# GpSimd's share of scaling duT: another instruction, and 1.5 chunks a step in the third to seventh segment

## The reference, cut to what matters

```python
dA = jnp.exp(delta[..., None] * A)
dBu = delta[..., None] * Bm[:, :, None, :] * u[..., None]
def step(h, inp):
    dA_t, dBu_t, C_t = inp
    h = dA_t * h + dBu_t
    y = jnp.einsum('bdn,bn->bd', h, C_t)
    return (h, y)
```

## Time and profile before

| | us |
|---|---|
| median of 3 runs (699.59 to 702.44) | 699.82 |
| span of the profiled execution | 716.2 |
| first product L564 starts | 60.4 |
| third segment's first product | 170.5 |
| eighth segment's first product | 461.5 |
| last product ends | 515.7 |

### The profile page before, as it was taken

The page is one execution under the profiler, slowest core; times in us unless marked ns, Lnnn a source line. Parts: engine busy times, 40 slices in busy tenths (PEclk is TensorE's granted clock), DMA queues, the critical chain, the costliest instruction groups (busy, mean ns, idle before and its releaser), DMA issues.

```text
span 716.2 us, 14511 instructions
## 1 busy us (share of the span) xinstructions
PE 619.3 (86%) x4435; PEld 514.5 (72%) x4435; DVE 551.1 (77%) x1170; ACT 542.8 (76%) x1023; POOL 512.8 (72%) x479
## 2 busy tenths in 40 slices
PE   3878789989979988998998995878798878899995
PEld 3435757857857767776786784767688878899994
DVE  4357689899999999989999999899954663555553
ACT  3268989989998998998998998889655543565650
POOL 3147969878899899899899999868735445444440
PEclk9999999999999999999999999899999999999997
DMA  7030534445734633553344533596112222222535
GB/s 231 2 118 2 139 89 151 112 127 166 233 103 133 170 103 102 147 156 105 99 121 132 141 101 102 156 238 163 39 47 58 59 56 65 62 67 62 166 123 184
DMA packets 65197, 82.93 MB, mean 116 GB/s; under 512 B 6961, under 2 KB 55153, under 8 KB 61025
## 3 DMA queue, kind: packets, MB, share of 16 engines
q1 hardware_dynamic: 59648, 70.78, 36.3%
q0 software_dynamic: 4320, 9.12, 3.8%
q10 hardware_dynamic: 1152, 2.10, 0.8%
HBM read 52.19 MB, written 29.78 MB: 114 GB/s over the span
## 4 chain that ended last, share of the span: by engine, by line
PE 40%; ACT 37%; DVE 11%; issue 8%; another core or an unknown queue 2%; DMA 2%; ACTq 0%; DVEq 0%; SPq 0%
PE psum L594 25%; PE psum L598 15%; ACT S L1019 13%; ACT dA L1027 12%; DVE ring L1383 4%; ACT L958 1%; ACT xn L923 1%; DMA ring<-results 1%; ACT L1027 1%; ACT soft L951 1%; ACT soft L950 1%; ACT soft L958 1%; ACT soft L955 1%; ACT hT L905 1%
## 5 line engine op out<-in xcount | busy, mean ns | idle before, releaser
L564 POOL TENSOR_TENSOR ring<-ring,Cb 128x1024 f32<-128x1024 f32 x128 | 279.9, 2188 | 37.2 <-DVE ring L1383 36.8
L598 PEld LDWEIGHTS psum<-ident,S 128*128 128x128 f32 x1024 | 118.7, 142 | 112.7 <-issue 66.4
L598 PE MATMUL psum<-ident,S 128*128 128x128 f32 x1024 | 158.8, 279 | 42.5 <-POOL S L547 13.7
L1019 ACT ACTIVATE S<-duT,BT 128x256 f32<-128x256 f32 x384 | 166.5, 502 | 25.3 <-DVE duT L1123 22.6
L1027 ACT ACTIVATE dA<-delta,A 128x512 f32<-128x512 f32 x256 | 178.7, 716 | 8.6 <-DVE ring L1383 8.5
L598 PE MATMUL psum<-ident,ring 128*128 128x128 f32 x1088 | 159.7, 278 | 5.4 <-DMA ring<-results 5.3
L1383 DVE TENSOR_TENSOR_SCAN ring<-dA,state,psum 128x512 f32<-128x512 f32 x128 | 157.7, 1265 | 1.0 <-PE psum L598 0.4
L1383 DVE TENSOR_TENSOR_SCAN ring<-dA,psum 128x512 f32<-128x512 f32 x128 | 150.1, 1206 | 8.8 <-PE psum L598 8.2
L586 POOL DMA_INDIRECT results<-xn,result_at x71 | 69.0, 972 | 92.2 <-DVE xn L1516 76.5
L598 PEld LDWEIGHTS psum<-ident,ring 128*128 128x128 f32 x1088 | 129.0, 144 | 6.7 <-DMA ring<-results 5.9
L594 PE MATMUL psum<-uT,S 128*128 128x128 f32 x852 | 109.7, 279 | 1.6 <-DVE uT L1494 1.2
(11 more groups left out here) (226 smaller groups left out, 739.0 us busy)
## 6 DMA issues: line engine op xcount, KB each, us to landing
Cb<-c_rows SPq DMA_DIRECT2D x32, 1024.0 KB, 6.0
token_rows<-zeros SPq DMA_DIRECT2D x64, 272.0 KB, 6.7
uT<-token_rows SPq DMA_DIRECT2D x71, 68.0 KB
ring<-results SPq DMA_DIRECT2D x8, 512.0 KB
xT<-in_xT SPq DMA_DIRECT2D x4, 512.0 KB, 5.4
out_T<-xT ACTq DMA_DIRECT2D x8, 256.0 KB, 2.3
stage<-in_xT SPq DMA_DIRECT2D x6, 256.0 KB, 7.8
gateup_w<-in_gate SPq DMA_DIRECT2D x1, 1408.0 KB, 10.3
```

The lines of the kernel that those rows point to most:

```text
L564: nc.gpsimd.tensor_tensor(ring[:, k % RING, :, 0:BANK], ring[:, k % RING, :, 1:], Cb[:, group_ % 2, own, :].unsqueeze(1).to_broadcast([P, ...
L598: return nc.tensor.matmul(out, block_in, ident[at, at], is_transpose=True, start=start, stop=True, skip_group_check=True)
L1019: nc.scalar.activation(S[:, k % S_SLOTS, c, :], duT[:, s % 2, c, :], ACT.Identity, scale=BT[:, s % 2, c, n:n + 1]).then_inc(scaled_act, 1)
```

## The change

POOL's multiplication by B becomes one `tensor_scalar` a chunk, with B as a per-partition scalar and a second operation, times 1.0, where it was one `tensor_tensor` of all its chunks, with B broadcast along the row. `pool_chunks` gives POOL 1 chunk in even and 2 in odd steps of all segments but the last, which still has none. The count that PE waits for follows. `add_bias` gets a neutral second operation too.

```diff
 def pool_chunks(k):
     s = k // NSTATE
-    return 1 + k % 2 if s < 2 else int(s < SEGS - 1)
+    return 1 + k % 2 if s < SEGS - 1 else 0
...
 def pool_scaled(k):
-    return sum(pool_chunks(j) > 0 for j in range(k + 1))
+    return sum(pool_chunks(j) for j in range(k + 1))
...
-                nc.gpsimd.tensor_scalar(xT[...], xT[...], gabo[:, b:b + 1], None,
-                                        ALU.add).then_inc(gabo_added, 1)
+                nc.gpsimd.tensor_scalar(xT[...], xT[...], gabo[:, b:b + 1], 1.0,
+                                        ALU.add, ALU.mult).then_inc(gabo_added, 1)
...
-                    nc.gpsimd.tensor_tensor(S[:, k % S_SLOTS, CS - own:, :], duT[:, s % 2, CS - own:, :],
-                                            BT[:, s % 2, CS - own:, n:n + 1].to_broadcast([P, own, MLP]), ALU.mult
-                                            ).then_inc(scaled_pool, 1)
+                    for c in range(CS - own, CS):
+                        nc.gpsimd.tensor_scalar(S[:, k % S_SLOTS, c, :], duT[:, s % 2, c, :], BT[:, s % 2, c, n:n + 1], 1.0,
+                                                ALU.mult, ALU.mult).then_inc(scaled_pool, 1)
```

More of the change, by code:

```diff
@@ L510, in add_bias @@
                 pool.wait_ge(stat_filled, SEG * (b + 1))
-                nc.gpsimd.tensor_scalar(xT[:, b * SEQ:(b + 1) * SEQ], xT[:, b * SEQ:(b + 1) * SEQ], gabo[:, b:b + 1], None,
-                                        ALU.add).then_inc(gabo_added, 1)
+                nc.gpsimd.tensor_scalar(xT[:, b * SEQ:(b + 1) * SEQ], xT[:, b * SEQ:(b + 1) * SEQ], gabo[:, b:b + 1], 1.0,
+                                        ALU.add, ALU.mult).then_inc(gabo_added, 1)
             def gap_work(gap, window):
```

## The result

The changed kernel takes 705.28 us (median of 5 runs, 703.52 to 707.78), the kernel before 700.98 (5 runs): a ratio of 1.0071, 95% interval 1.0052 to 1.0090. It is slower by 4.3 us by the medians (5.0 by the ratio). The forecast was 5.3 us faster, counted from the 699.8 us known then, and the time lies outside the range of 685.4 to 704.0.

What follows compares the result with a forecast made beforehand. ACT was taken to bound segment heads, ACT and POOL the rest. Waits removed, -6.0 us, plus POOL's added work, +0.6, gave -5.4, as median -5.3: 699.8 to 694.5 us, range 685.4 to 704.

Steps and rivals of the forecast that it cites:

- The bound: Third to seventh segment: ACT sets the pace at each head, ACT and POOL both full in the other two thirds.
- ACT's relief, -16.0 us: Odd steps of five segments: ACT loses 40 L1019 instructions at 0.40 us each, 16.0 us in all.
- POOL's chunk: POOL's scaling in the new form: 430 ns a chunk, 0.385 us of pitch, +0.6 us over five segments.
- The upper value of 451 ns: POOL's 256-element chunk, estimated from L501 with its slope raised by 1.21; +3.6 us over five segments.
- The rival of a slow form: POOL's scaling: the per-partition scalar makes a chunk 770 to 880 ns, giving 728 to 742 us; chance 0.13.
- The waits that ACT's relief was to remove: Segment heads: of POOL's 12.9 us of waits for the scan, 1.2 us a segment go, 6.0 in five.
- The rival "POOL is the wall already": Third to seventh segment: ACT's 16 us become longer waits at the turn; gain 0 to 3 us, chance 0.23.
- "POOL works two steps ahead, so only the mean counts.": PE's wait for POOL's counts: a pair's +0.20 us and even steps' -0.19 average out, unless POOL is behind.
- a cap reached about twice a segment: POOL's chunk stands two steps ahead at most, limiting the scan's lead; read from PE's 13.7 us of waits.
- add_bias, zero: Before 50 us: add_bias falls from 2872 ns to 1.1 to 1.3 us, with no gain as nobody waited.
- A reading of L547: POOL's existing scaling: it held 604 to 621 ns beside a busy DVE, supporting added chunks on POOL.
- The median from the span: Whole kernel: the median is 0.977 of the 716.2 us profiled span, turning -5.4 us into -5.3.

Runs made afterwards that it cites:

- e5: Changed kernel with one POOL chunk a step in the third to seventh segment, plus a POOL scaling into a spare tile in odd steps; 706.26 us, ratio 1.0076.
- e11: Kernel before with POOL's scaling three steps ahead of the product instead of two, nothing else; 695.85 us, ratio 0.9947.
- e4: Changed kernel with two POOL chunks only in steps 1, 3 and 5 of the third to seventh segment, one in their other steps; 698.67 us.
- e1: Changed kernel with the new instruction but one POOL chunk a step in the third to seventh segment, as before; 699.36 us, ratio 0.9978.
- e3: Changed kernel with the second chunk of odd steps in the third to seventh segment computed by neither ACT nor POOL; 695.34 us, ratio 0.9925.
- e6: Changed kernel with the constant 0.5 in place of the per-partition scalar in POOL's scaling; 700.76 us, ratio 1.0001.
- e9: Changed kernel with POOL's scaling three steps ahead of the product instead of two; 698.22 us, ratio 0.9971.
- e10: Changed kernel with one POOL chunk a step in the third to seventh segment and POOL's scaling three steps ahead; 695.42 us, ratio 0.9937.

## Why the prediction was wrong, point by point

**The bound.** It read POOL as the wall in two thirds of each segment and ACT at the head. The first half held only for the order of work as it stood (e5: POOL's work alone makes the changed kernel's stretch): e11 takes 3.5 us off the stretch without making POOL shorter. The second half did not hold: e4 relieves ACT at the head and gains 0.6 us in the stretch over e1.

**ACT's relief, -16.0 us.** The amount was right. The busy time fell by 13.2 us (270.8 to 257.6), but the window of the changed kernel holds 37 instructions fewer and not 40; e3, with the same relief, has 15.4 us less than e1.

**POOL's chunk, the first term that was mis-sized.** 430 ns and 0.385 us of pitch were taken; it is 476 ns, and a pair takes 0.90 us from start to start, 0.45 each. The term of 120 x 0.385 - 45.6 = +0.6 us is 120 x 0.45 - 45.6 = +8.4. Measured, POOL's work grew by 9.8 us; 0.9 of the other 1.4 are idle time before scatters (5.7 to 6.6), and the rest is not accounted for. The slope from L501 was right (476 to 1140 ns for 256 to 1024 elements is 0.865 ns an element, 0.85 had been read). What failed is the fixed part: L501 has immediates, and the per-partition scalar adds 69 ns (e6), which was nobody's term. The upper value of 451 ns was too low for the same reason, as its factor of 1.21 was put on the slope alone. The rival of a slow form was priced a little low (770 to 880 ns; with one operation it is 924), and rejected rightly: it is the missing operation that makes it, and the per-partition scalar adds only its 69 ns.

**The waits that ACT's relief was to remove, -6.0 us, the step that failed.** POOL's waits did fall, by 4.9 us, but e5 has the same fall without the relief: a longer POOL fills its own waits, at no gain. The test is e6, where POOL's work is that of the kernel before to 0.1 us and ACT's relief is whole: POOL's waits are 12.6 us against 12.9, the time is that of before (ratio 1.0001). So with the chunk's cost as forecast the change would have brought nothing, not 5.4; whether the later second chunk of a pair hides a small gain stays open (e6). The rival "POOL is the wall already" (a gain of 0 to 3 us, 0.23) was the true one for that part, at its end of no gain, and the range had held it. In the stretch the forecast had -6.0 + 0.6 = -5.4 us; measured were -4.9 of waits and +9.8 of work, +4.9. The 4.9 that looks like the forecast gain is what the longer POOL itself filled.

**"POOL works two steps ahead, so only the mean counts."** This sentence was wrong and hid the cause. The two steps are eaten by the product and the scatter in front of the chunk, even with POOL waiting 18.8 us (e1), and a third step gives 3 to 7 us (e9, e10, e11). PE's 13.7 us of waits for POOL's S in the earlier trace rows had been read as a cap reached about twice a segment. By the ends PE waited 28.0 us in 27 waits, over five a segment, and they went when the chunk was moved ahead at unchanged length (e11, 0.2 us). They were the sign of a late place in POOL's queue.

**add_bias, zero.** 2872 to 1140 ns, and the start of the scan moved from 60.4 to 60.1 us: no gain that counts, as forecast.

**A reading of L547.** The "604 to 621 ns" are the smallest value and the median over all 112 instructions; single chunks went up to 660 ns. Nothing in the sum rests on it. The slow form's upper time, 742 us, is 741 by its own sum.

**The median from the span.** The factor of 0.977 came of the disturbed tail of the profile; it changed the forecast by 0.1 us.

**What stays open.** Why ACT's relief of 16 us is worth 2.4 us in the stretch where POOL is light (e3) was not taken apart further. PE waits 21.5 us for POOL's late chunk there too, and DVE, 268 us busy of 287, and PE, 262, are near the whole stretch, but no run shows which it is. The run that would tell, the whole relief with the scaling three steps ahead and POOL light, was not made.

## What to carry to other kernels

Where engine A waits for B's small piece and B has idle time of its own, look at what stands in front of the piece in B's queue before making B shorter: here the move of one line brought 4 us to the kernel before, and 22% off the piece's length (618 to 481 ns) brought 1.6 in the stretch. Before a wait in the list is believed, look at what ended just ahead of it: here 14 us of waits for POOL stood under other names. An exchange of work between engines pays only if the receiver's price is measured in the form and at the size used; a cost that a small neighbour doesn't have (here the per-partition scalar's) decides when instructions are short. When waits of the receiver are to disappear, name who ends them: they also disappear, at no gain, when the receiver gets longer.

## What the runs showed of the hardware

- On POOL a tensor_scalar of f32 with a per-partition scalar and one operation costs 924 ns for 256 elements and 2872 for 1024, 2.54 ns an element; with a second one that changes nothing, 476 and 1140, 0.865 ns an element. The fixed parts, by the two sizes, are about 275 and 255 ns.
- The per-partition scalar costs 69 ns over an immediate at 256 elements with two operations (476 against 407 ns, 168 instructions each). No run has it at another size.
- PE starts 0.10 us after the end of the POOL scaling that it waited for (27 waits of the kernel before, 28 of the changed one). An indirect DMA of 128 rows holds POOL for 1.0 us (L473, 64 of them, mean 1019 and 1034 ns).
- The Trainium skill (GPSIMD Engine Reference, section 3.1) has 1.03 cycles an element at 1.2 GHz, by estimate 0.86 ns, for a body of at most two operations; the form with two operations agrees (0.865), that with one does not.
